# Score products as two halves of four 32-row products, and the expert rows fetched tile by tile inside the second self-attention

## What is computed

```
x = x + tanh(g0) * cross_attention(layernorm(x), ctx)       # 16 heads of 8, blocks of 64
h = layernorm(x)
for l in (0, 1):
    h = h + attention(ln1(h))                               # 16 heads of 8, causal
    m = ln2(h)
    h = h + (token_moe(m) if l == 0 else seq_moe(m))        # 8 experts, the best two
x = x + tanh(f0) * h
x = x + tanh(g1) * mlstm(layernorm(x), ctx)                 # 8 heads of 16, gates from x and ctx
x = x + tanh(f1) * int8_linear(layernorm(x))
```

## Time and profile before

| | before |
|---|---|
| median of 3 timed runs | 1274.37 us (1271.04 to 1277.46) |
| the profiled execution | 1265.2 us |
| its span, first to last instruction | 1263.5 us |
| PE busy | 980.7 us, 78% |
| DVE busy | 836.2 us, 66% |
| ACT busy | 700.8 us, 55% |
| POOL busy | 584.5 us, 46% |
| mean granted clock of PE | 0.854 |

### The profile page before, as it was taken

One profiled execution on the slowest core, in us unless ns is written; L12 is line 12 of the kernel. 1 busy time (PEld: TensorE's weight loads), 2 busy tenths in 40 slices (PEclk: granted clock), 3 DMA queues, 4 the chain that ended last, 5 costly groups with the idle time before them and its releaser, 6 DMA issues.

```text
span 1263.5 us, 30781 instructions
## 1 busy us (share of the span) xinstructions
PE 980.7 (78%) x9835; PEld 759.3 (60%) x9835; DVE 836.2 (66%) x1984; ACT 700.8 (55%) x1780; POOL 584.5 (46%) x804
## 2 busy tenths in 40 slices
PE   4999998999974899993005999965999978899503
PEld 2677676677674799993003777744777758555301
DVE  4599998999848566661425999976222245389874
ACT  2577677878730177772004777743555522588643
POOL 6355544655620255554773666612333310378423
PEclk9899999999965599997556999966999995699855
DMA  4000040000020022221214000000000001011102
GB/s 124 12 13 15 15 137 2 2 0 0 1 67 0 17 67 64 65 65 47 53 52 134 2 0 0 1 2 0 0 0 0 0 25 50 7 47 44 30 0 67
DMA packets 51918, 38.74 MB, mean 31 GB/s; under 512 B 6072, under 2 KB 45476, under 8 KB 51860
## 3 DMA queue, kind: packets, MB, share of 16 engines
q1 hardware_dynamic: 46956, 28.88, 7.8%
q0 software_dynamic: 4320, 8.86, 2.7%
q10 hardware_dynamic: 584, 0.26, 0.1%
HBM read 29.13 MB, written 8.85 MB: 30 GB/s over the span
## 4 chain that ended last, share of the span: by engine, by line
PE 48%; DVE 12%; issue 11%; ACT 9%; POOL 7%; POOLq 7%; DVEq 3%; DMA 2%; SPq 1%; ACTq 0%
PE ps_s L1000 9%; PE ps_o L1000 8%; PE ps_t L1084 7%; PE ps_v L1000 6%; PE ps_a L1000 5%; PE ps_t L1000 5%; POOLq L688 5%; POOL h_all L659 2%; POOL w L659 2%; ACT work L811 2%; POOL work L689 2%; DVEq L1599 2%; PE ps_v L1104 1%; POOLq L678 1%; PE ps_x L1039 1%
## 5 line engine op out<-in xcount | busy, mean ns | idle before, releaser
L632 POOL TENSOR_TENSOR kbd<-kts,kmask 128x512 f32<-128x512 f32 x192 | 240.9, 1276 | 223.1 <-ACT qts L797 140.8
L652 POOL DMA_INDIRECT xg<-x_rows,row_from x71 | 73.5, 1036 | 137.8 <-DVE slot_of L1592 70.1
L819 ACT COPY probs_t<-ps_t 128x1024 f32<-128x1024 f32 x96 | 97.2, 1012 | 68.4 <-PE ps_t L1084 68.4
L1427 DVE TENSOR_REDUCE rowmax<-ps_s 128x16 f32<-128x1024 f32 x96 | 116.5, 1213 | 17.0 <-PE ps_s L1000 16.9
L1000 PE MATMUL ps_s<-kbd,qts 64*64 64x512 f32 (+1 forms) x1024 | 124.6, 559 | 0.2 <-issue 0.2
L1430 DVE TENSOR_TENSOR work<-ps_s,rowmax 128x1024 f32<-128x1024 f32 x96 | 117.6, 1225 | 3.3
L1000 PE MATMUL ps_o<-vst,probs_t 128*64 128x18 f32 x3072 | 108.5, 214 | 5.3 <-ACT probs_t L819 5.3
L1000 PEld LDWEIGHTS ps_o<-vst,probs_t 128*64 128x64 f32 x3072 | 98.9, 139 | 17.6 <-ACT probs_t L819 6.9
L1039 PE MATMUL ps_x<-ident,xn 128*128 128x128 f32 x96 | 31.1, 323 | 100.8 <-DVE xn L1418 100.8
L1084 PE MATMUL ps_t<-ident,work 128*128 128x128 f32 x768 | 103.5, 279 | 7.2 <-ACT work L811 5.7
L811 ACT ACTIVATE work<-work 128x1024 f32<-128x1024 f32 x96 | 100.9, 1051 | 1.3 <-DVE work L1430 1.2
(11 more groups left out here) (370 smaller groups left out, 2382.2 us busy)
## 6 DMA issues: line engine op xcount, KB each, us to landing
y_rows<-work SPq DMA_DIRECT2D x71, 64.0 KB, 1.6
w<-in_L_ffn_e_w_dram SPq DMA_DIRECT2D x2, 2048.0 KB, 8.6
ctx_dup<-in_ctx_dram SPq DMA_DIRECT2D x64, 64.0 KB, 2.3
x_res<-in_x_dram SPq DMA_DIRECT2D x4, 512.0 KB, 6.6
ctx_in<-in_ctx_dram SPq DMA_DIRECT2D x32, 64.0 KB, 1.8
x_rows<-h_all SPq DMA_DIRECT2D x1, 2048.0 KB, 9.2
work<-in_ctx_dram SPq DMA_DIRECT2D x8, 256.0 KB, 2.7
out_dram<-work SPq DMA_DIRECT2D x16, 128.0 KB, 1.8
```

The lines of the kernel that those rows point to most:

```text
L632: i = pool.tensor_tensor(km[:, par, g, :, :], kts[:, par, g:g + 1, :].to_broadcast([P, 8, SEQ]), kmask[:, :, :], ALU.mult)
L652: pool.indirect_dma_start(xg[:, t % XBUFS, :], None, x_d, bass.IndirectOffsetOnAxis(row_from[:, t:t + 1], 0)).then_inc(xg_loaded[t % XBUFS ...
L819: nc.scalar.copy(probs_t[:, par, :], ps_t[:, :]).then_inc(S["pts_ready"], 1)
L1427: V.tensor_reduce(rowmax[:, par, :], s3, AXX, ALU.max).then_inc(S["max_ready"], 1)
```

## The change

1. Keys are spread in groups of 4 heads in 32 rows (`HPG = 4`) instead of 8 in 64. `kbd` and `kmask` have half the columns, and POOL's `kbd_step` is one instruction instead of two.
2. The scores of a tile are eight products of 32 rows x 64 queries x 256 columns, in two steps. `scores` has four of them, in four row groups, two of which write different partitions of each bank. `other_scores` has the four others and waits for the first four's results (`half_scored`). The transposes of ctx and x stand between the two steps. The causal mask is two products of 64 rows x 128 columns x 512 in place of four.
3. DVE's `norm_step` has lag 0 and is the last step of the iteration.
4. The fetches become a step of the second self-attention, with a ring of 16 semaphores. Combining and sums follow 4 to 6 iterations behind, the statistics come in four groups of eight tiles, and the attention's steps lag 15 iterations behind the fetches. ACT, not DVE, normalises (`normalise`, after exp). ACT, DVE and POOL run this stage unrolled (`straight`).
5. In the gates stage all context groups come first, then all x groups; the square root moves behind the copies of the context groups.
6. POOL makes one more constant and builds `kmask` in four parts.

```diff
+def straight(steps, hooks=(), n=NT):
+    hooks = dict(hooks)
+    for i in range(n + max(step[0] for step in steps)):
+        if i in hooks:
+            hooks[i]()
+        for step in steps:
+            t = i - step[0]
+            if 0 <= t < n:
+                step[1](t, t % 2, *(t % buffers for buffers in step[2:]))
...
-                    for g in range(SPT):
-                        i = pool.tensor_tensor(km[:, par, g, :, :],
-                                               kts[:, par, g:g + 1, :].to_broadcast([P, 8, SEQ]),
-                                               kmask[:, :, :], ALU.mult)
-                    i.then_inc(S["kbd_ready"], 1)
+                    pool.tensor_tensor(km[:, par, :, :, :],
+                                       kts[:, par, :, :].unsqueeze(2).to_broadcast([P, SPT, HPG, SEQ]),
+                                       kmask[:, :, :].unsqueeze(1).to_broadcast([P, SPT, HPG, SEQ]), ALU.mult
+                                       ).then_inc(S["kbd_ready"], 1)
...
-            for t in range(NT):
-                fetch(t)
-            pipeline(pool, [(2, kbd_step(ATT[1])), (3, bias_step(1))])
+            straight(later([(2, kbd_step(ATT[1])), (3, bias_step(1))], LEAD) + [(0, fetch)])
...
+            straight(later(attention(1, 1), LEAD) + [(LEAD, normalise)],
+                     {GROUP * g + LEAD - 1: lambda g=g: row_std(CH_SELF1 + g, GROUP * g, GROUP * (g + 1))
+                      for g in range(NGROUP)})
...
+            def score_products(t, par, turned, masked):
+                for u in range(GROUPS):
+                    q, r, at = (u + turned) % SPT, u // 2, u % 2 * HPG * SEQ
+                    h_ = slice(32 * u, 32 * u + 32)
+                    yield mm(ps_s3[64 * q:64 * q + 64, r, at:at + HPG * SEQ], qts[h_, par, q * SEQ:(q + 1) * SEQ],
+                             km[h_, par, q, :, :].rearrange("p h k -> p (h k)"), not masked, True)
...
+                    for r in range(2 if masked else 0):
+                        h_ = slice(64 * r, 64 * r + 64)
+                        mm(ps_s3[:, r, :], ident_seqs[h_, :, :].rearrange("p s q -> p (s q)"),
+                           causal[h_, :, :].rearrange("p a b -> p (a b)"), True, False)
+                    for i in score_products(t, par, 0, masked):
+                        i.then_inc(S["half_scored"], 1)
...
+                    pe.wait_ge(S["half_scored"], GROUPS * (ATT[base] + t + 1))
...
                 return [(L_SCORES, scores(base, l is not None)),
+                        (1, ctx_transpose(base)) if l is None else None, (1, transposes(base, nbase)),
+                        (L_SCORES, other_scores(base, l is not None)),
                         (L_OUT, transpose_y(base)), (L_WEIGH, transpose_probs(base)),
-                        (2, project(base, l)), (1, ctx_transpose(base)) if l is None else None,
-                        (1, transposes(base, nbase)), (L_OUT, out_project(base, l)), (L_WEIGH, weigh(base), VBUFS)]
+                        (2, project(base, l)), (L_OUT, out_project(base, l)), (L_WEIGH, weigh(base), VBUFS)]
...
             for g in range(NB + 1):
                 if g < NB:
                     context_group(g)
+                if g:
+                    context_gates(g - 1)
+            for g in range(NB + 1):
+                if g < NB:
                     x_group(g)
                 if g:
-                    i = gates_group(g - 1)
+                    i = x_gates(g - 1)
...
-                return [(L_OUT, y_step(base)), (1, norm_step(src, nbase, base, norm)),
-                        (L_SCORES, shift_step(base)), (L_OUT + 1, sums_step(dst, "x_updated", UPD[base])),
-                        (L_OUT, add_step(base, dst, scale))]
+                return [(L_OUT, y_step(base)), (L_SCORES, shift_step(base)),
+                        (L_OUT + 1, sums_step(dst, "x_updated", UPD[base])), (L_OUT, add_step(base, dst, scale)),
+                        (0, norm_step(src, nbase, base, norm))]
...
+            straight(later(attend[:-1], LEAD)
+                     + [(4, combine_first), (5, combine_second), (6, sums_step(inner, "second_done", 0, "stats_done"))], hooks)
```

More of the change, by code:

```diff
@@ L50 @@
 MAGIC = 12582912.0
+GROUP = 8
+NGROUP = NT // GROUP
+LEAD = GROUP + 7
+RING = 16
 ROW0_PAIRS = 3.0
@@ L107, with later @@
 SEAM = 4
+def straight(steps, hooks=(), n=NT):
[7 more added lines that the diff above has]
+                step[1](t, t % 2, *(t % buffers for buffers in step[2:]))
+def later(steps, lag):
+    return [(step[0] + lag,) + tuple(step[1:]) for step in steps if step]
 def chained(eng, segments, hooks=(), n=NT, unroll=4):
@@ L564, in routing_constants @@
                 select(identb[:, :], [[-1, P]], 0, 1, ALU.not_equal, 1.0)
+                fresh(pool.memset(ident_seqs[:, :, :], 0.0))
+                for half in range(2):
+                    part = ident_seqs[half * 64:(half + 1) * 64, :, :]
+                    select(part, [[0, SPT], [-1, SEQ]], 0, 1, ALU.not_equal, 1.0)
                 fresh(pool.memset(causal[:, :, :], 0.0))
@@ L886, in _, with normalise @@
             pipeline(act, [(1, turn_affine), (2, turn_gelu, XBUFS)], NTURN)
-            row_std(CH_SELF1)
-            pipeline(act, [step for step in attention(1, 1) if step])
+            def normalise(t, par):
+                if t % GROUP == 0:
+                    act.wait_ge(S["nbias_ready"], 2 + t // GROUP + 1)
+                seen(act, S["xt_ready"], TB[1] + t - 1)
+                nc.scalar.activation(xn[:, par, :], tile(inner, t), ACT.Identity, bias=nbias[:, t:t + 1],
+                                     scale=rstd[:, t:t + 1]).then_inc(S["xn_ready"], 1)
+            straight(later(attention(1, 1), LEAD) + [(LEAD, normalise)],
+                     {GROUP * g + LEAD - 1: lambda g=g: row_std(CH_SELF1 + g, GROUP * g, GROUP * (g + 1))
+                      for g in range(NGROUP)})
             row_std(CH_PRE1)
@@ L920, in _ @@
                 nc.scalar.copy(inner[:, g * BLK:(g + 1) * BLK], (ps_o, ps_v)[g % 2][:, :]).then_inc(S["cg_sb"], 1)
+            row_std(CH_MLSTM)
+            for g in range(NB):
                 act.wait_ge(S["xg_tr"], g + 1)
@@ L1065, in fn, with other_scores @@
                     pe.sem_inc(S["scores_begun"], 1)
[L1066 to L1075 removed]
+                    for r in range(2 if masked else 0):
[4 more added lines that the diff above has]
+                        i.then_inc(S["half_scored"], 1)
+                return fn
+            def other_scores(base, masked):
+                def fn(t, par):
+                    pe.wait_ge(S["half_scored"], GROUPS * (ATT[base] + t + 1))
+                    pe.sem_inc(S["scores_begun"], 1)
+                    for i in score_products(t, par, 1, masked):
+                        pass
                     i.then_inc(S["scores_ready"], 1)
@@ L1264, in x_group, with context_gates, x_gates @@
                 i.then_inc(S["xg_tr"], 1)
-            def gates_group(g):
+            def context_gates(g):
                 pe.wait_ge(S["cg_sb"], g + 1)
+                for t in range(g * SUB, (g + 1) * SUB):
+                    mm(ps_t[:, t * 16:(t + 1) * 16], tile(inner, t), wg_t[:, 1, :], False, False)
+            def x_gates(g):
                 pe.wait_ge(S["xg_sb"], g + 1)
                 for t in range(g * SUB, (g + 1) * SUB):
-                    mm(ps_t[:, t * 16:(t + 1) * 16], tile(inner, t), wg_t[:, 1, :], False, False)
                     i = mm(ps_t[:, t * 16:(t + 1) * 16], tile(h_t, t), wg_t[:, 0, :], False, True)
@@ L1385, in row_means @@
                 c = slice(a, b)
-                dve.wait_ge(S["bn_done"], need)
+                dve.wait_ge(S[done], need)
                 even, odd = stats[:, c, 1], stats[:, c, 4]
```

94 lines of the change are left out of this document (43 added, 51 removed).

## The result

| | median | runs | profiled execution | span | granted clock |
|---|---|---|---|---|---|
| before | 1273.3 us | 1271.0 to 1277.5 (4) | 1265.2 us | 1263.5 us | 0.854 |
| changed | 1286.1 us | 1281.0 to 1288.3 (4) | 1281.0 us | 1279.3 us | 0.871 |

The ratio is 1.0091, with a 95% interval of 1.0049 to 1.0133: the change makes the kernel slower, by some 12 us (6 to 17 by the interval). The prediction said 1270 us and gave "faster" the largest chance. The time lies in its range, 1244 to 1298 us, but the direction is wrong.

A forecast was written before the change was run, and what follows sets the result against it. Bounds: PE's own work, loops between two engines, and the fetch window. Sum 8.1 + 4.6 - 53.8 + 43.0 - 6 = -4.1 us: profile 1265.2 to 1261, plus 9 to the median, 1270 us; range 1244 to 1298.

The forecast's parts named there:

- Score products: Halved products in the first two attentions: +0.30 us a tile in cross (+8.1 us), 4.96 to 5.13 in self (+4.6 us).
- switch: On PE, a change to products of another shape costs 0.15 us without streaming.
- covers: Between the halves on PE, the 0.26 us transpose of x hides the 0.15 us a result takes to leave the array.
- (2): Rival on PE: changes of product shape cost next to nothing, 12.7 us of the first two attentions go, 1258 us; chance 0.10.
- (4): Rival on PE: row groups writing one bank wait for each other, 0.435 us more a half, 1329 us; chance 0.06.
- (5): Rival on POOL: kbd with two broadcasts runs at half the rate, 2.5 us, 1335 us; chance 0.05.
- (3): Rival on PE: each half costs 0.2 us more, 1298 us; the sign turns above 0.62 us a half; chance 0.12.
- Start of the second self-attention: Fetch window: only 34 fetches precede the first kbd, so the first masked product starts at 626.0, not 679.84: -53.8 us.
- The loop through normalise: Second self-attention: ACT waits for PE after `normalise`, 5.92 us a tile against 4.69; +43.0 us with ramps and statistics.
- rival (1): Second self-attention: the wait through `normalise` is hidden, PE's own 5.13 us a tile holds, 1248 us; chance 0.12.
- events: Three statistics groups inside the second self-attention, adding DVE instructions, a table load and reciprocals: 2.6 us each, 7.8 in all.
- Gates: Gates stage: eight context groups run while PE would stand waiting for the statistics, -6 us (bounds 0 and -15).

## Why the prediction was wrong

**What bounds the kernel:** right. PE in the steady attentions and the fetch window were the two places, and work on either moved the time.

**Score products:** the mechanism was right, the sizes were not. The half of 0.585 us was measured at 0.59. The prediction read a switch of 0.15 us from the chain of waits, whose rows give the first of several transposes 0.26; the timeline gives it 0.17. It charged 0.15 each to the second half, the mask and the output projection, and nothing to the transpose of x. In the self-attentions (before at 750 us, changed at 303 us) the timelines show +0.22 for the scores (0.96 to 1.18), +0.08 for the mask (0.24 to 0.32), +0.10 for the output projection (0.32 to 0.42) and +0.17 for the transpose of x (0.16 to 0.33). The last holds the wait for the first half's results, 0.33 us and not the 0.15 that "covers" assumed. Together that is +0.57 where +0.45 was forecast, with errors to both sides; in the cross attention it is +0.36 for +0.30. By its end the last subtraction is 8.8 us late (forecast 8.1), and the late first one (3.05 us) is part of that, since the intervals behind it are shorter than before. The first self-attention adds 7.6 us (forecast 4.6), and so +12.7 became +16.4. Rivals (2), (4) and (5) fall with the rows of a tile; kbd with two broadcasts is no slower than its old single instruction: the page of the changed kernel has 1277 ns as its mean, that of before 1276. For (3), the halves' own price, 0.59 lies just under its turning point of 0.62.

**Start of the second self-attention:** -53.8 became -48.0. From the first fetch to the first subtraction it is 46.4 us less (101.4 to 54.9); the other 1.5 us lie ahead of the fetches, in a stage that varies by 3 us from kernel to kernel. The 34 leading fetches took 42.2 us, as forecast. The missing step is ACT's stand, 6 to 7 us. No row of before shows ACT working beside fetches, and the prediction took their neighbours to be undisturbed.

**The loop through normalise:** its mechanism was foreseen, at 5.92 us, and measured, at 5.99; rival (1) falls. The four items added to 4.96 make 1.00, not 0.96, so the sum should have read 5.96. What failed is the price of the events and ramps on top of it: +43.0 became +54.5. Of the 11.5 us of difference the events have 5.7: three of 2.6 us were added as if PE went on at full clock, but in this loop an event drops the clock, and 7.8 became 13.5; where the loop is gone it is 6.4. The first three intervals have 3.3 (they cost 6.3 us more than in the kernel before, not 3), the steady tiles 1.7, the last three 0.9. The prediction named a sinking clock as what would make it wrong, and gave it no time.

**Gates:** -6 against -7.2 in the profiles, right.

**From span to median:** I carried over the 9 us between profile and median of before. For the changed kernel they are 5. This hid 4 us: the profile is 20 us above its forecast (1281 for 1261), the median only 16 (1286 for 1270). That is luck.

**The sign:** the forecast was a small difference of two large sums, -60 of gains and +56 of costs. They came out at -55 and +71, and so 4 us of gain in the profile became 16 of loss, 13 by the medians. A forecast so built deserved more than 0.29 for slower: of its unknowns (a wait, contention with the fetches, clock, ramps) nearly all could only cost.

## What to carry to other kernels

A step put into another engine's order can close a loop: write the round trip down, and try the step first and last in that order; here that alone was worth 29 us. An instruction made half as wide pays only where another engine waits for it; halves and small kbd paid under the fetches and cost 0.3 to 0.6 us a tile elsewhere, so a layout can differ from stage to stage. When a sum is small beside its terms, ask of each unknown to which side it can err.

## What was not expected of the hardware

- Dependent products of the same operand shape need 0.92 us from start to start where the work is 0.59: results reach PE's next waiting instruction 0.33 us after the last one could follow.
- ACT stood still for 11.8 us beside a run of indirect fetches, 9.8 of them after its input was ready. A pause of 5.0 us on POOL removed the stand and cost nothing, and behind the pause ACT worked beside running fetches without one. The mechanism is open.
- A loop with 0.74 us of idle PE a tile keeps the 2.4 GHz level in the changed kernel, but each of the three events on top of it dropped the clock: 0.75 over 19 us, 0.86 over 24 us and 0.89 over 16 us. The window between the first two, asked for PE alone:

```profile
692.00:720.00 28.00, 24.36 (x349) 1.00 0.09 23
```
